# The fourth batch runs three steps behind the third in the second front block

## The chip, the cores and the metric

The kernel runs on one core of one Trainium2 chip. The metric is the device time of one execution in microseconds (us); lower is better. All data are float32, apart from a few small tables.

## What is computed

The reference is a stack of four layers over x (4 batches, 512 tokens, width 128), each with a gated cross-attention to a context of 32 tokens and a gated feed-forward part:

```python
x = x + tanh(g_xattn[0]) * L0_xattn(layernorm(x), ctx, ...)   # one head, 32 keys
x = x + tanh(g_ffn[0])   * L0_ffn(layernorm(x), ...)          # MXFP4 rounding, then one 128x128 product
x = x + tanh(g_xattn[1]) * L1_xattn(layernorm(x), ctx, ...)   # 16 heads, 32 keys
x = x + tanh(g_ffn[1])   * L1_ffn(layernorm(x), ...)          # router, top 2 of 8 experts
x = x + tanh(g_xattn[2]) * L2_xattn(...)                      # layers 2 and 3: the other 1,580 us
...
```

The change touches only the stage that computes the first three of these lines for the last two batches. The attention of layer 1 is the part that matters most below:

```python
scores = einsum('bqhd,bkhd->bhqk', q, k) / sqrt(8)            # 16 heads of 8
scores = where(mask == 0, -1e9, scores)
out = einsum('bhqk,bkhd->bqhd', softmax(scores), v)           # then @ Wo + bo
```

## The kernel before

The program is a sequence of blocks; all engines meet at the end of each. The first block computes the "front" (the three lines above) of batches 0 and 1 beside the setup. The **second front block**, `fronts_beside_route` (L3102 to L3123), computes the front of batch 2 (the third) and batch 3 (the fourth), and beside them the router of the first two batches, `route_1` with g = 0, whose last act is 16 indirect DMAs that scatter token rows to the experts' pages. The third block, `moe_1_pages`, works on those pages.

The order of every engine's queue is fixed by `interleave` (L749). Each part of the work is written, for each engine, as a generator that yields step numbers. The first part is the main one (here the third batch), the others are sides. Before the main part's code of a step, all sides with a due step no later than it are advanced, the lowest due first, and at equal dues the side named first. What the sides have left after the main part follows at the end. So with equal step numbers the fourth batch goes just ahead of the third at every step on every engine. The router runs at two front steps for one of its own; its 16 scatters (L1240) are due on POOL from step 20 in half steps.

Engines are in order: an instruction that waits holds all behind it. One front (`front`, L794) has these steps, by name of the product in PSUM: `kv` (0, from the context), `xt0` and `q0` (2, 3), `sc0` (5, scores of layer 0), `vo`, `vo1` (6, 7), `pt0`, `y0` (8, 9, output of layer 0's attention), quantisation on DVE (12 to 15, L416 to L434), `xt1`, `y1` (17, 18), `xt2`, `q1` (21, 22), and then the layer-1 attention over four token tiles t:

- `sc1_t` (23+t): PE makes the scores (L890), DVE takes them out of PSUM with a minimum (L1041) and reduces the maximum (L1044);
- POOL subtracts it (L1093, from step 23), ACT takes the exponential (L951, from 24), DVE sums and inverts (L1049 and L1050, from 25), POOL multiplies (L1098, from 25);
- `pt1_t` (27, 28, 30, 31): PE transposes (L898), ACT copies (L955);
- `v1_0` (29) and `v1_1` (32): PE multiplies by the values (L904, 16 products), DVE adds bias and residual (L1055, L1058).

A front has one PSUM bank, so each product of a batch waits until the one before it has been taken out (`free_for`, on the semaphore `taken`). The two fronts have banks and buffers of their own. In the trace the third batch's tiles are called rows, turned, small_f and x; those of the fourth weights, ysb, region_a, work and pt. Layer norms take statistics on DVE (L664, L667), an inverse root on POOL (L674, L675, `norm_rstd`, steps 0, 10, 19) and the application on DVE (L685). POOL also widens keys and values to all heads (L1074, L1079).

`paced` (L3066) wraps a side so that every step it yields goes through a function; it exists and is used in a later block.

Of the kernel before, what the change touches and what calls it, by code (L numbers as in the profile page):

```python
# [63 lines left out]
def record(**fields):  # L64

    return namedtuple("Record", fields)(**fields)


def flamingo_kernel(nc, a, at, early_at, out):
    with ExitStack() as ctx:  # L70
# [4 lines left out]
        def sems(parity, names, behind=None):  # L75

            first = behind.end if behind else 0
            for n in range(len(sem_sets[parity]), first + len(names)):
                sem_sets[parity].append(ctx.enter_context(nc.semaphore(f"{'even' if parity == 0 else 'odd'}_{n}")))
            return record(end=first + len(names), **dict(zip(names, sem_sets[parity][first:])))  # L80
# [17 lines left out]
        def bank(i, n=1):  # L98
            return psum[:, 512 * i:512 * (i + n)]
# [12 lines left out]
        def part(region, offset, shape):  # L112

            n = int(np.prod(shape[1:]))
            v = region[0:shape[0], offset:offset + n]
            if len(shape) == 3:
                v = v.rearrange("p (a b) -> p a b", a=shape[1])
            if len(shape) == 4:
                v = v.rearrange("p (a b c) -> p a b c", a=shape[1], b=shape[2])
            return v  # L120
# [194 lines left out]
        def next_inputs(n):  # L315
            return dict(ctx_tok=lg[0:K, 2 * n:2 * n + 2, :].rearrange("p t e -> p (t e)"), ctx_t=lge[:, n, 0:K],
                        mask0=lge[:, n, K:2 * K].bitcast(I32),
                        mask1=comb[:, 2 * n:2 * n + 2, :].rearrange("p t (h k) -> p (t h) k", h=2).bitcast(I32))

        front_3, front_4 = dict(front_1, **next_inputs(0)), dict(front_2, **next_inputs(1))  # L320
        w_at = front_tail + FRONT_SMALL
        front_w2 = record(stats=part(region_a, w_at, [P, T, 6]), mv=part(region_a, w_at + 24, [P, T, 2]),
                          rstd=part(region_a, w_at + 32, [P, T]), rtmp=part(region_a, w_at + 36, [P, T]),
                          rstd2=part(region_a, w_at + 40, [P, T]), xn=part(work, 0, [P, T, D]), xnt=part(wide_2, 3584, [P, S]))
# [87 lines left out]
        def over(ap, axis, shape):  # L412
            return ap.unsqueeze(axis).broadcast_to(shape)
# [349 lines left out]
        def block_of(k, sync, main, sides, first_loads=None):  # L763

            with nc.Block() as block:  # L765
                @block.sync
                def _(sp):
                    if first_loads:
                        first_loads(sp)
                    clear_set(sp, 1 - k % 2)  # L770
                    sync(sp)

                @block.tensor
                def _(pe):
                    interleave(main.tensor(pe), [side.tensor(pe) for side in sides])

                @block.scalar
                def _(act):
                    interleave(main.scalar(act), [side.scalar(act) for side in sides])

                @block.vector
                def _(dve):
                    interleave(main.vector(dve), [side.vector(dve) for side in sides])

                @block.gpsimd
                def _(pool):
                    interleave(main.gpsimd(pool), [side.gpsimd(pool) for side in sides])
# [461 lines left out]
        def load_pages(sp, s, q):  # L1249
            lo = 4 * P * (q % QUADS)  # L1250
            sp.dma_start(page_rows[:, q % 3, :, :],
                         sorted_1[q // QUADS][lo:lo + 4 * P, :].rearrange("(j p) d -> p j d", p=P)).then_inc((s.in_0, s.in_1, s.in_2)[q % 3], 16)
# [1813 lines left out]
        def paced(side, at_step):  # L3066

            def slowed(program):
                def of_engine(eng):
                    for n in program(eng):  # L3070
                        yield at_step(n)
                return of_engine
            return record(tensor=slowed(side.tensor), vector=slowed(side.vector), scalar=slowed(side.scalar),
                          gpsimd=slowed(side.gpsimd))
# [3 lines left out]
        def next_block():  # L3078
            block_at[0] += 1
            return block_at[0]  # L3080
# [21 lines left out]
        def fronts_beside_route():  # L3102
            k = next_block()
            sf = sems(k % 2, FRONT)
            sg = sems(k % 2, FRONT, sf)
            sr = sems(k % 2, ROUTE_1, sg)
            sw = sems(k % 2, ("table_in",), sr)
            s_pages = sems(1 - k % 2, PAGES_1)

            def sync(sp):  # L3110
                sp.wait_ge(sf.inputs, 5 * 16)
                sp.wait_ge(sg.inputs, 5 * 16)
                lo = early_at["b1"][0]
                sp.dma_start(w1[D - 1:D, :, 0:F1],
                             a["early"][0:E8, lo:lo + F1].rearrange("(o e) f -> o e f", o=1)).then_inc(sw.table_in, 16)
                lo = at["be2"][0]
                sp.dma_start(be2_rows[:, :, :], over(a["weights"][0:E8, lo:lo + D], 0, [P, E8, D])).then_inc(sw.table_in, 16)
                sp.wait_ge(sw.table_in, 32)
                sp.wait_ge(scattered_1[0], 16 * K1 * GT)
                for q in range(3):  # L3120
                    load_pages(sp, s_pages, q)
            block_of(k, sync, front(sf, 2, bank(0), front_3, set_f),
                     [front(sg, 3, bank(1), front_4, front_w2), route_1(sr, 0, bank(2), lambda n: 2 * n, 4)])  # L3123

        def moe_1_pages():
            k = next_block()
# [99 lines left out]

        fronts_beside_setup()
        fronts_beside_route()
        moe_1_pages()
        for b in range(B):  # L3230
# [122 lines left out]
```

## Time and profile before

| | us |
|---|---|
| median of 3 runs | 1809.48 |
| lowest, highest | 1801.71, 1815.31 |
| time of the profiled execution | 1816.59 |
| its span | 1814.8 |
| second front block in it | 115.7 to 230.1 |

The profiled execution was 7.1 us above the median of the runs. All stretches are in us from the start of its span. The engines are PE (matmul), PEld (its weight load), DVE (vector), ACT (scalar), POOL (GpSimd) and SP (which issues plain DMAs). The busy shares of the whole span say little here, since most of it lies in later blocks; what the change touches is one stretch of 114.4 us, and it has to be read by itself.

### The profile page before, as it was taken

How to read it: one execution, taken by the hardware profiler on the slowest of the kernel's cores; microseconds unless marked ns; L12 is line 12 of the kernel's file. 1: busy time of each engine (PE TensorE's matmuls, PEld its weight loads, DVE VectorE, ACT ScalarE, POOL GpSimd, SP SyncE). 2: the span in 40 equal slices, each digit the busy share in tenths (PEclk: the TensorE clock that was granted, in tenths of full speed). 3: DMA queues.
4: the chain of work that ended last, by engine and by line, in shares of the span. 5: the costliest groups of instructions: out<-in, count | busy, mean ns of one | idle time of the engine just before them, and what ended most of it. 6: DMA issues, size and time to landing. Idle time of an engine off the chain costs nothing. (4 is left out here: it accounts for less than half of the span.)

```text
span 1814.8 us, 30972 instructions
## 1 busy us (share of the span) xinstructions
PE 1594.1 (88%) x10175; PEld 1088.8 (60%) x10175; DVE 1175.5 (65%) x3120; ACT 772.7 (43%) x1974; POOL 850.9 (47%) x1075
## 2 busy tenths in 40 slices
PE   5655599899999999999999997968999999788799
PEld 4545376657756567655577564545656765567655
DVE  6867577857747467575577564476847757445557
ACT  2321244446627466355465273122226626533421
POOL 2551734538647277474486562011727647400072
PEclk7875799999999999999999997879999999899899
DMA  8200122100000400000000001014410000434363
GB/s 300 79 13 1 41 83 77 42 10 10 1 1 2 162 13 4 1 1 1 5 9 1 1 2 47 1 46 135 144 33 2 1 18 1 148 91 117 94 161 115
DMA packets 79564, 91.34 MB, mean 50 GB/s; under 512 B 10872, under 2 KB 57592, under 8 KB 78480
## 3 DMA queue, kind: packets, MB, share of 16 engines
q1 hardware_dynamic: 74288, 78.86, 13.9%
q0 software_dynamic: 5120, 10.50, 2.0%
q8 instruction: 86, 1.41, 0.3%
q14 instruction: 70, 0.57, 0.1%
HBM read 69.14 MB, written 27.66 MB: 53 GB/s over the span
## 5 line engine op out<-in xcount | busy, mean ns | idle before, releaser
L1677 POOL TENSOR_TENSOR rows<-rows,rinv 128x512 f32<-128x512 f32 x192 | 198.7, 1063 | 117.2 <-DVE rinv L1917 117.2
L1841 ACT ACTIVATE rows<-psum,nmax 128x512 f32<-128x512 f32 x192 | 130.0, 683 | 122.1 <-DVE nmax L1910 122.0
L2026 POOL TENSOR_TENSOR rows<-rows,rinv 128x128 f32<-128x128 f32 (+2 forms) x192 | 127.4, 685 | 76.5 <-DVE rinv L2195 76.5
L1909 DVE TENSOR_REDUCE lg<-psum 128x2 f32<-128x1024 f32 x128 | 155.7, 1217 | 3.2
L2190 DVE TENSOR_REDUCE nmax<-psum 128x1 f32<-128x128 f32 (+3 forms) x256 | 113.6, 486 | 41.7 <-PE psum L2072 40.7
L1921 DVE COPY turned<-psum 128x512 f32<-128x512 f32 x128 | 88.2, 689 | 80.3 <-PE psum L1737 79.3
L1725 PE MATMUL psum<-region_a,region_b 64*128 64x256 f32 x1024 | 130.6, 391 | 6.0 <-ACT rows L1841 2.9
L1758 PE MATMUL psum<-turned,region_a 128*64 128x256 f32 x1024 | 124.6, 385 | 0.4
L2069 PE MATMUL psum<-region_a,region_b 64*128 64x128 f32 (+2 forms) x896 | 105.9, 349 | 10.5 <-ACT rows L2142 4.6
L1725 PEld LDWEIGHTS psum<-region_a,region_b 64*128 64x128 f32 x1024 | 92.8, 186 | 28.9 <-ACT rows L1841 7.7
L1737 PEld LDWEIGHTS psum<-weights,rows 128*128 128x128 f32 x768 | 82.0, 140 | 44.9 <-issue 20.7
L1737 PE MATMUL psum<-weights,rows 128*128 128x128 f32 x768 | 103.3, 279 | 3.9 <-ACT turned L1850 2.4
L2142 ACT ACTIVATE rows<-psum,nmax 128x128 f32<-128x128 f32 (+2 forms) x192 | 96.1, 509 | 11.2 <-DVE nmax L2190 11.2
L2584 ACT ACTIVATE region_b<-psum 128x512 f32<-128x512 f32 x66 | 39.4, 598 | 139.7 <-PE psum L2546 139.7
L1758 PEld LDWEIGHTS psum<-turned,region_a 128*64 128x64 f32 x1024 | 68.6, 136 | 47.1 <-issue 19.6
L1850 ACT ACTIVATE turned<-psum 128x512 f32<-128x512 f32 x128 | 76.7, 599 | 46.0 <-PE psum L1737 46.0
L2069 PEld LDWEIGHTS psum<-region_a,region_b 64*128 64x128 f32 x896 | 69.4, 188 | 34.6 <-ACT rows L2142 11.9
L2558 PEld LDWEIGHTS psum<-region_c,region_b 128*128 128x128 f32 x512 | 66.0, 192 | 28.0 <-issue 22.7
L2084 PE MATMUL psum<-weights,rows 128*128 128x128 f32 x448 | 76.3, 280 | 6.6 <-DVE region_a L2201 1.4
L1703 PE MATMUL psum<-kvt,weights 128*128 128x512 f32 x128 | 66.1, 646 | 11.2 <-PEq L765 7.6
L2850 POOL DMA_INDIRECT sorted<-turned,small_f x48 | 49.2, 1024 | 49.6 <-DVE small_f L2784 35.2
L1689 POOL TENSOR_TENSOR ysb<-ysb,nmax 128x128 f32<-128x128 f32 x64 | 25.9, 405 | 94.8 <-DVE nmax L1910 93.9
(866 smaller groups left out, 3962.0 us busy)
## 6 DMA issues: line engine op xcount, KB each, us to landing
pt<-gates SPq DMA_DIRECT2D x64, 128.0 KB, 3.1
ysb<-gates SPq DMA_DIRECT2D x64, 128.0 KB, 3.1
weights<-sorted SPq DMA_DIRECT2D x28, 256.0 KB, 3.0
made<-weights SPq DMA_DIRECT2D x28, 256.0 KB, 2.3
sorted<-sorted SPq DMA_DIRECT2D x4, 1536.0 KB, 13.7
region_a<-in_eg SPq DMA_DIRECT2D x16, 256.0 KB, 4.4
region_a<-in_eu SPq DMA_DIRECT2D x16, 256.0 KB, 3.9
region_c<-in_weights SPq DMA_DIRECT2D x16, 256.0 KB, 5.7
```

The lines of the kernel that those rows point to most:

```text
L1677: nc.gpsimd.tensor_tensor(row(u, j), row(u, j), rinv[:, 2 * u + j:2 * u + j + 1].broadcast_to([P, S]), ALU.mult).then_inc(s.pn, 1)
L1725: mm = nc.tensor.matmul(s_bank(u, j)[:, 256 * half:256 * (half + 1)], qtt[lo:lo + 64, p, P * t:P * (t + 1)], ktt[lo:lo + 64, p, 256 * half ...
L1737: mm = nc.tensor.transpose(turn_bank(place(n, i))[:, P * k:P * (k + 1)], row(u, j)[:, P * k:P * (k + 1)], ident[:, :])
L1758: nc.tensor.matmul(bank(7)[lo:lo + HD2, 256 * half:256 * (half + 1)], vtok[:, k, P * p + lo:P * p + lo + HD2], turned2[:, 2 * half + j, k, :],
L1841: nc.scalar.activation(row(u, j), s_bank(u, j), ACT.Exp, bias=nmax[:, 2 * u + j:2 * u + j + 1], accum_out=sum_column(u // T, u % T, j)).th ...
L1850: nc.scalar.activation(turned_to(n, i), turn_bank(place(n, i)).rearrange("p (k q) -> p k q", q=P), ACT.Copy).then_inc(s.ca, 1)
L1909: link(nc.vector.tensor_reduce(maxima(u // T)[:, both(u), 0], both_scores(u), AX.X, ALU.max, negate=True))
L1921: nc.vector.tensor_copy(turned_to(n, i), turn_bank(place(n, i)).rearrange("p (k q) -> p k q", q=P)).then_inc(s.cb, 1)
L2026: nc.gpsimd.tensor_tensor(head, head, rinv[:, 2 * u + j:2 * u + j + 1].broadcast_to([P, keys(u)]), ALU.mult).then_inc(s.pn, 1)
L2069: nc.tensor.matmul(s_bank(u, j)[:, cols], qtt[lo:lo + 64, p, P * t:P * (t + 1)], krot[lo:lo + 64, cols], start=(h == 0), stop=True, skip_g ...
L2142: nc.scalar.activation(rows_of(u)[:, j, 0:keys(u)], s_bank(u, j)[:, 0:keys(u)], ACT.Exp, bias=nmax[:, 2 * u + j:2 * u + j + 1], accum_out= ...
L2190: nc.vector.tensor_reduce(nmax[:, 2 * u + j:2 * u + j + 1], s_bank(u, j)[:, 0:keys(u)], AX.X, ALU.max, negate=True).then_inc(s.mx, 1)
```

## The change

The fourth batch's front is wrapped in `paced` with `lambda n: n + 3`: on every engine but SP, its step n is due where the third batch's step n + 3 was. No instruction is added, removed or altered; only the order within the queues of PE, ACT, DVE and POOL is another.

```diff
@@ -3120,7 +3120,7 @@
                 for q in range(3):
                     load_pages(sp, s_pages, q)
             block_of(k, sync, front(sf, 2, bank(0), front_3, set_f),
-                     [front(sg, 3, bank(1), front_4, front_w2), route_1(sr, 0, bank(2), lambda n: 2 * n, 4)])
+                     [paced(front(sg, 3, bank(1), front_4, front_w2), lambda n: n + 3), route_1(sr, 0, bank(2), lambda n: 2 * n, 4)])
```

The POOL queue at the end of the block, by this rule (3 and 4 are the batches, D the scatters, sub L1093, mul L1098):

```
before: 4:rstd 3:rstd D0-D5 4:sub0 D6 3:sub0 D7 4:sub1 D8 3:sub1 D9 4:sub2 4:mul0 D10 3:sub2 3:mul0 D11
        4:sub3 4:mul1 D12 3:sub3 3:mul1 D13 4:mul2 D14 3:mul2 D15 4:mul3 3:mul3
after:  3:rstd D0-D3 4:rstd D4-D6 3:sub0 D7 D8 3:sub1 D9 D10 3:sub2 3:mul0 D11 4:sub0 D12 3:sub3 3:mul1
        D13 4:sub1 D14 3:mul2 D15 4:sub2 4:mul0 3:mul3 4:sub3 4:mul1 4:mul2 4:mul3
```

The ends of the other queues after the change:

```
PE:  3:pt1_0 4:sc1_2 3:pt1_1 4:sc1_3 3:v1_0 4:pt1_0 3:pt1_2 4:pt1_1 3:pt1_3 4:v1_0 3:v1_1 4:pt1_2 4:pt1_3 4:v1_1
ACT: 3:copy0 4:exp1 3:copy1 4:exp2 4:exp3 4:copy0 3:copy2 4:copy1 3:copy3 4:copy2 4:copy3
DVE: 3:sum2 4:max2 4:sum0 3:sum3 4:max3 4:sum1 3:v1_0 4:sum2 4:sum3 4:v1_0 3:v1_1 4:v1_1
```

## Rows read from the trace of the kernel before

**Rows 1.** The page, part 1: busy time, share and instructions of each engine.

```profile
PE 1594.1 (88%) x10175; PEld 1088.8 (60%) x10175; DVE 1175.5 (65%) x3120; ACT 772.7 (43%) x1974; POOL 850.9 (47%) x1075
```

**Rows 2.** Windows: stretch, length, busy time and count by engine, granted clock, DMA share.

```profile
115.70:230.10 114.40, 64.79 (x298) 48.37 (x298) 77.43 (x272) 23.02 (x49) 51.31 (x70) 0.67 0.07 21
...
115.70:158.60 42.90, 26.17 (x132) 20.87 (x132) 29.01 (x130) 9.67 (x26) 16.17 (x34) 0.63 0.05 13
158.60:182.00 23.40, 9.39 (x42) 8.93 (x42) 20.46 (x86) 1.40 (x3) 1.27 (x2) 0.57 0.00 0
186.20:222.80 36.60, 23.36 (x79) 13.16 (x78) 21.43 (x38) 10.26 (x17) 32.60 (x32) 0.74 0.09 29
```

**Rows 3.** Waits of DVE in the block: total us, times, longest.

```profile
DVE weights L1006 <- PE psum L858: 4.6, 1, 4.6
DVE kvt L1153 <- POOL kvt L1227: 3.7, 1, 3.7
...
DVE small_f L993 <- PE psum L839: 2.1, 1, 2.1
```

**Rows 4.** Timeline of POOL: start, duration, instruction; first scatter, last multiplication.

```profile
184.69 0.23 POOL L674 TENSOR_SCALAR rtmp_f<-mv_f 128x4 f32<-128x4 f32 x1 [3.68 <-DVE mv_f L667]
185.00 1.03 POOL L675 TENSOR_TENSOR rstd_f<-rtmp_f,neg_half 128x4 f32<-128x4 f32 x1
186.24 1.29 POOL L1240 DMA_INDIRECT sorted<-region_c,slots  x1 [0.20 <-issue]
...
221.69 1.05 POOL L1098 TENSOR_TENSOR rows<-rows,small_f 128x512 f32<-128x512 f32 x1
```

**Rows 5.** POOL's instructions by line, 182 to 223.5: busy us, mean ns, idle before.

```profile
L1240 POOL DMA_INDIRECT sorted<-region_c,slots x16 | 16.0, 1002 | 3.4 <-issue 3.4
L1093 POOL TENSOR_TENSOR rows<-rows,small_f 128x512 f32<-128x512 f32 x4 | 4.2, 1057 | 0.1
```

**Rows 6.** Timeline of DVE: quantisation's start, the third batch's step 18, the end.

```profile
158.51 0.68 DVE L420 TENSOR_REDUCE region_a<-y 128x16 f32<-128x512 f32 x1
...
181.94 0.69 DVE L1025 TENSOR_TENSOR turned<-psum,weights 128x512 f32<-128x512 f32 x1
...
184.52 1.08 DVE L685 TENSOR_SCALAR work<-weights,region_a 128x128 f32<-128x128 f32 x4
...
229.59 0.48 DVE L1058 SCALAR_TENSOR_TENSOR x<-turned,gate,x 128x256 f32<-128x256 f32 x1
```

**Rows 7.** Timeline of PE: transposes and value products at either clock.

```profile
215.19 1.12 PE L898 MATMUL psum<-weights,rows 128*128 128x128 f32 x4 [2.12 <-ACT turned L955]
216.10 3.39 PE L904 MATMUL psum<-weights,ysb 128*128 128x128 f32 x16
219.33 1.95 PE L904 MATMUL psum<-rows,turned 128*128 128x128 f32 x16
...
224.77 0.66 PE L898 MATMUL psum<-weights,rows 128*128 128x128 f32 x4 [0.25 <-ACT turned L955]
```

**Rows 8.** Timeline of ACT: an exponential and a copy.

```profile
214.02 0.63 ACT L951 ACTIVATE rows<-rows 128x512 f32<-128x512 f32 x1 [2.12 <-POOL rows L1093]
...
225.46 0.60 ACT L955 ACTIVATE turned<-psum 128x512 f32<-128x512 f32 x1 [0.26 <-PE psum L898]
```

**Rows 9.** Timeline of DVE: two operations, each once short and once long.

```profile
130.16 0.18 DVE L974 TENSOR_SCALAR pt<-region_a 128x32 f32<-128x32 f32 x1
...
131.57 0.97 DVE L974 TENSOR_SCALAR pt<-cap3s 128x32 f32<-128x32 f32 x1
...
219.99 3.04 DVE L1058 SCALAR_TENSOR_TENSOR weights<-pt,gate,weights 128x256 f32<-128x256 f32 x1
...
227.80 0.49 DVE L1058 SCALAR_TENSOR_TENSOR weights<-pt,gate,weights 128x256 f32<-128x256 f32 x1
```

**Rows 10.** Windows, columns as in rows 2: the granted clock late in the block.

```profile
206.00:210.00 4.00, 1.54 (x7) 0.76 (x5) 2.48 (x6) 0.63 (x1) 3.77 (x5) 0.50 0.05 16
...
222.00:226.00 4.00, 2.33 (x18) 2.03 (x19) 1.85 (x3) 1.97 (x4) 0.74 (x1) 1.00 0.65 191
```

## The prediction

> **What bounds the kernel now.** I began with the page. Its busy line [rows 1] shows PE busy for 88% of the span, but that is a mean over stages; the changed block is 114.4 us of 1814.8, so I cut it out with the windows view and left the rest. In the block [rows 2] no engine is full: PE 64.8 us, DVE 77.4, POOL 51.3, ACT 23.0. The later lines of that group cut it into three stages.
>
> - 115.7 to 158.6: DVE works 29.0 of 42.9 us. The 13.9 us in which it rests are chains through other engines: 3.7 us for POOL's iota at the start, 2.1 and 4.6 us for PE products [rows 3].
> - 158.6 to 182: DVE works 20.5 of 23.4 us. Quantisation of both batches and the router stand one behind the other; DVE is the bound.
> - 186.2 to 222.8: POOL shows 32.6 us of work in 36.6, and the rest is issue gaps between scatters (16.0 us of work and 3.4 of gaps for 16 of them [rows 5]). POOL is the bound. Its first scatter starts at 186.24 only because both inverse roots, the third batch's at 185.00, stand in front of it; its last multiplication starts at 221.69 [rows 4]. After that 7.3 us of transposes, copies and value products follow, up to 230.07 on DVE [rows 6].
>
> So the block's end is: DVE's work up to the layer norm of layer 1, then POOL's queue, then a tail.
>
> **The change, part by part.** Nothing is added, so all terms are changes of waits. I walk the four new queues with the durations of the rows.
>
> *First stage.* The router's iota now comes first on POOL, and DVE's 3.7 us wait for it shrinks to 0.7: 3.0 gained. The third batch's chain then runs without the fourth's to fill its waits: an inverse root costs 0.31 + 1.03 = 1.35 us from statistics to application [rows 4], now exposed twice (2.8 us with hand-overs), and some 0.8 us for the context's chain. Later the fourth's `sc0`, `vo` and `y0` each stand in PE's queue behind two to four products of the third and the router; I get DVE waits of 2.0, 3.1 and 3.0 us where the waits of before were 2.1, 0.7 and 4.6 [rows 3]. In all 13.9 us of waits (0.7, 2.8, 0.8, 8.1, and 1.5 of small ones) against 12.4 that I count by the same standard: with hand-overs about +1.7 us. This is the term I trust least. I bound it below by -3.7 (the whole wait for the iota falls away and nothing comes for it) and above by +4.6 (one more product wait as long as the longest).
>
> *Second stage.* DVE is full, so order costs nothing here. Before, DVE started quantising at 158.51 and reached the third batch's step 18 at 181.94 [rows 6], 23.4 us later, with the fourth's step 18 of 2.6 us and a wait of 1.3 us ahead of it. Afterwards the fourth's step 18 comes behind the third's and the wait is gone, so the third's step 18 starts at 158.5 + 1.7 + 23.4 - 2.6 - 1.3 = 179.7. Its 2.6 us (181.94 to 184.52) and the inverse root of 1.35 end at 183.7. POOL's first scatter starts there, at 183.9 with the hand-over: 2.3 us earlier than 186.24.
>
> *POOL's queue.* A scatter costs (16.0 + 3.4) / 16 = 1.21 us, a subtraction or multiplication 1.05 [rows 5]. From 183.9: four scatters (4.8), the fourth batch's inverse root (1.35), now inside this run, then twelve scatters (14.5) and thirteen tensor operations (13.7) up to the fourth's last subtraction: 218.3. I checked that inputs are there. The tightest is the fourth's last maximum: PE makes its `sc1_3` only behind the third's `pt1_1`, which needs mul1 of the third at about 208.8, so the maximum is ready near 212.5 and POOL asks for it at 217.2. 4.7 us of cover hide that link; if they are gone, each us goes to the end. Three multiplications remain, to 221.4, against 222.7 before: POOL is done 1.3 us earlier.
>
> *The tail.* Here the lag is paid. ACT's queue holds the fourth's exp3 in front of its copy0 and of the third's copy2, so no `pt1` after the first of the fourth leaves PSUM before 218.3 + 0.63 (exp) + 0.60 (copy0) = 219.6 [rows 8]. Then in PE's order: the fourth's pt1_1 (1.1 at the low clock), the third's pt1_3 (1.1), the fourth's v1_0 (3.4 low), the third's v1_1 (1.95 high) [rows 7], which ends near 227.3. Then alone, with nothing beside them: pt1_2 0.66, copy 0.60, pt1_3 0.66, copy 0.60, v1_1 1.95, DVE's two operations 0.95, and five hand-overs of about 0.1. Sum 227.3 + 5.4 + 0.3 = 233.0, against 230.1. The tail behind POOL's last operation grows from 7.3 to 11.6 us.
>
> SP's page loads of the next block wait for the last scatter, which comes about 6 us earlier. That is worth nothing, since PE starts the next block at the meeting of the engines.
>
> **Sum.** POOL's start: +1.7 (first stage) -2.6 -1.3 (the fourth's step 18 and the wait, no longer ahead) = -2.2, with hand-overs -2.3. The inverse root inside the run: +1.35. The 0.4 us that POOL waited before its first subtraction: -0.4. So POOL's end: -1.3. The tail: 11.6 - 7.3 = +4.3. Together +3.0, and 233.0 against 230.07 is +2.9; I take +2.9. Against the profiled execution, 1816.59 + 2.9 = 1819.5; against the median of the runs, which lay 7.1 us lower, 1809.5 + 2.9 = **1812.4 us**.
>
> **Clock.** The granted clock was 0.50 (1.2 GHz) from 206 to 210, where PE worked 1.5 of 4 us, and 1.00 (2.4 GHz) from 222 to 226 [rows 10]; the first 16 value products took 3.39 us, the next 1.95 [rows 7]. I let the first `v1` of the closing run be slow and the rest fast, as there. With all of the tail fast the end is 2.4 us earlier (+0.5 instead of +2.9), with all of it slow 3.8 later (+6.7). The Trainium skill (TensorE: Matmul & The Clock Gate, Part 1) says that a gate halves the array's clock depending on how busy PE has been; by that rule the thinner PE work of a lagged tail speaks for the slow side, and the trace agrees (0.50 in the thin stretch).
>
> **Rivals.**
>
> *The lag pays (faster by a few us).* POOL is the bound of the last stage and starts 2.3 us earlier; if the tail overlaps well, only the fourth's pt1_3, copy, v1_1 and DVE's part follow its last multiplication (0.66 + 0.60 + 1.95 + 0.95 + hand-overs = 4.6): 221.8 + 4.6 = 226.4, so -3.7, 1805.8 us. For it: POOL at 32.6 of 36.6 us [rows 2]. Against it: ACT's order, exp3 ahead of copy0. A second mechanism speaks against it: DVE operations on SBUF alone were stretched while POOL ran tensor operations, 0.18 to 0.97 us and 0.49 to 3.04 us [rows 9]. The third's `v1_0` addition (L1058) would now fall into POOL's densest run with the fourth's sum2 and sum3 behind it; a stretch of 3 us brings POOL's end to about 224.8 and this rival to -0.7 us. In my own sum it is hidden, since PE asks for the fourth's mul3 only near 228.6. The Trainium skill (GPSIMD Engine Reference, Key points) says that GpSimd shares its SBUF interfaces with VectorE and contends with VectorE instructions that have two SBUF inputs or a 2-port mode; the trace agrees with both long rows.
>
> *The queues lock each other (clearly slower).* The place is PE's queue at the third's pt1_1 and the fourth's sc1_3, with DVE's `v1_0` ahead of sum2. It decides once the fourth's last maximum is later than 217.2, that is once more than 4.7 us are lost: then POOL stands idle. The price is what is over that, plus the slow tail (3.8): +6 to +10 us, 1815.5 to 1819.5. A cap for it: if the lag were pure addition, three steps of 33 in 114.4 us are 10.4 us.
>
> *No lag in time.* The order changes, but where every queue waits for the same chains both batches finish as before: within 1 us, 1809.5. For it: 77.4 us of DVE work in 114.4 is the same work; against it: the change in POOL's and ACT's order is real.
>
> **How the numbers follow.** Chances: my sum (+1 to +6) 0.50; the lag pays 0.20; lock 0.17; no shift 0.13. With the first stage at -3.7 instead of +1.7 and a fast tail my sum is 2.9 - 5.4 - 2.4 = -4.9; with +4.6 and a slow tail it is 2.9 + 2.9 + 3.8 = +9.6. And the three runs lay 7.8 us below to 5.8 above their median, so a median can be off by some 4 either way. From 1809.5 - 4.9 - 4 = 1800.6 to 1809.5 + 9.6 + 2 = 1821: I take 1801 to 1821. One per cent, about what a measurement can tell from no change, is 18.1 us; no case reaches it, with 10.4 the largest. So within 1% has 0.93; 0.03 faster and 0.04 slower are left for effects in later blocks that I do not see.
>
> **What would show it.** Right: the first scatter near 184, POOL's last multiplication between 221 and 223, the block's end near 233, a tail of 10 us or more after POOL, and ACT's copy of the fourth's first transposes directly behind its exp3. A first scatter later than 186.2 would put the first-stage term wrong; gaps over 1 us in POOL's run would show the lock; an end before 229 would show that the lag pays. The whole is wrong if blocks after 233 change by more than the shift itself.

## The result, and the profile after

The changed kernel took 1819.15 us (median of 13 runs, 1814.03 to 1822.42); the kernel before, now with 13 runs on the same chip, 1800.85 us (1798.39 to 1815.31). The ratio, over which the interval is given, is 1.0072 (95%: 1.0047 to 1.0098): 13 us slower, 8.5 to 17.6. The two medians themselves lie 18.3 us apart, so the size on this chip is not well known. On another chip a second comparison gave 1.0045 (1.0017 to 1.0073), or 8.6 us of 1912.7. The time lies in the forecast range and within 1%, but the forecast shift was 2.9 us and the measured one is three times that on the later chip and more than four times on the first.

The windows view of the changed kernel, first the block, then the stretches that answer to those of [rows 2] (columns: stretch, length, busy us and count of PE, PEld, DVE, ACT, POOL, granted clock, DMA share, GB/s). The block runs from the last DVE operation of the first block, 114.13, to PE's first product of the next at 232.54.

```profile
114.10:232.50 118.40, 74.61 (x298) 54.20 (x298) 80.02 (x272) 22.87 (x49) 51.53 (x70) 0.61 0.07 21
114.10:157.00 42.90, 30.78 (x127) 25.18 (x128) 26.46 (x116) 9.37 (x25) 15.13 (x32) 0.54 0.05 13
157.00:180.30 23.30, 10.44 (x43) 8.74 (x42) 20.79 (x89) 1.57 (x4) 1.26 (x2) 0.50 0.00 0
184.50:223.50 39.00, 25.46 (x74) 13.31 (x75) 27.39 (x52) 10.74 (x18) 33.86 (x34) 0.68 0.15 48
```

By the same marks the block took 230.38 - 115.70 = 114.7 us before and 232.54 - 114.13 = 118.4 after: +3.7. The mean granted clock fell from 0.67 to 0.61; in the second stage it was 0.50 throughout. PE's busy time rose by 10 us for the same products. The timeline of POOL in the changed kernel shows the earliest scatter and the end of its queue:

```profile
184.56 1.29 POOL L1240 DMA_INDIRECT sorted<-region_c,slots  x1 [0.20 <-issue]
...
219.15 1.03 POOL L1098 TENSOR_TENSOR weights<-weights,region_a 128x512 f32<-128x512 f32 x1
221.43 2.05 POOL L1098 TENSOR_TENSOR weights<-weights,region_a 128x512 f32<-128x512 f32 x2 [1.25 <-DVE region_a L1050]
```

The first scatter stands 70.4 us into the block; in [rows 4] it was 70.5. POOL ends at 109.4 instead of 107.0, and it waited 1.25 us for DVE ahead of its last two multiplications. The timeline of DVE shows why:

```profile
215.24 0.42 DVE L1055 TENSOR_TENSOR turned<-psum,weights 128x256 f32<-128x256 f32 x1 [0.42 <-PE psum L904]
215.70 4.77 DVE L1058 SCALAR_TENSOR_TENSOR x<-turned,gate,x 128x256 f32<-128x256 f32 x1
220.39 0.67 DVE L1049 TENSOR_REDUCE region_a<-weights 128x16 f32<-128x512 f32 x1
```

The addition of the third batch's `v1_0` took 4.77 us while POOL ran tensor operations (such an addition took 0.49 us in [rows 9] when POOL was done), and the fourth's sum2 stood behind it.

### The profile page after: what moved, and what is told of

Same layout as the page of the kernel before. It is cut to its first block and busy times, and to the rows that moved or that the text cites. A ratio compares the mean times of both kernels' runs of the same rounds, so it can differ in the third digit from the quotient of the medians.

```text
span 1813.0 us, 30977 instructions
## 1 busy us (share of the span) xinstructions
PE 1598.5 (88%) x10175; PEld 1090.4 (60%) x10175; DVE 1177.9 (65%) x3120; ACT 771.6 (43%) x1974; POOL 847.1 (47%) x1075
## 5 line engine op out<-in xcount | busy, mean ns | idle before, releaser
L2142 ACT ACTIVATE rows<-psum,nmax 128x128 f32<-128x128 f32 (+2 forms) x192 | 96.0, 509 | 11.6 <-DVE nmax L2190 11.6
L2850 POOL DMA_INDIRECT sorted<-turned,small_f x48 | 49.1, 1023 | 50.8 <-DVE small_f L2784 36.5
L2545 PE MATMUL psum<-xnt,region_a 128*128 128x512 f32 x128 | 68.0, 613 | 2.9 <-DVE region_b L2622 2.9
```

What stands on the lines that cost most here:

```text
L2142: nc.scalar.activation(rows_of(u)[:, j, 0:keys(u)], s_bank(u, j)[:, 0:keys(u)], ACT.Exp, bias=nmax[:, 2 * u + j:2 * u + j + 1], accum_out= ...
```

## Experiments

All figures of a block are counted from the last DVE operation of the first block to PE's first product of the next one. The kernels below ran on three other chips than the first comparison; there every kernel, the one before included, is about 100 us longer (last section), so only ratios and blocks are compared. A block is read from one profiled execution. The intervals of all kernels with three steps of lag overlap, so the ratios do not rank them.

| kernel | block us | ratio to before | 95% interval |
|---|---|---|---|
| before, three profiles | 114.7, 110.7, 110.7 | | |
| lag 3, three profiles | 118.4, 118.9, 118.8 | 1.0045 | 1.0017 to 1.0073 |
| lag 1, two profiles | 110.1, 110.0 | 0.9985, 0.9970 | 0.9962 to 1.0007, 0.9951 to 0.9989 |
| lag 3 early only | 121.1 | 1.0047 | 1.0024 to 1.0071 |
| lag 3 late only | 114.3 | 1.0014 | 0.9989 to 1.0038 |
| lag 3, PE filled from 158 us | 118.5 | 1.0039 | 1.0012 to 1.0065 |
| lag 3, PE filled at the start | 118.0 | 1.0032 | 1.0017 to 1.0046 |
| lag 3, addition from PSUM | 118.3 | 1.0027 | 1.0009 to 1.0044 |
| before, end delayed | 117.7 | 1.0026 | 1.0011 to 1.0040 |

### Is the profile of before typical, and does a later block pay?

The block had become 3.7 us longer between the two profiles at hand, the kernel 13 us by the runs. Two theories: later blocks answer to the shift through TensorE's clock, which changes often in them (A), or the front blocks themselves vary and the profile of before was an unlucky sample (B). Both kernels were profiled again, unchanged.

> The kernel before, unchanged, for one more profile of it. Its 13 runs fall into two groups, 9 of 1798.4 to 1801.7 us and 4 of 1807.9 to 1815.3, and the profile at hand is of the second. Theory A (the block costs 4 us and later blocks answer to the shift through TensorE's clock): a profile of the 1800 group has the second front block as long as before, 114 us within 1, and is shorter somewhere between 1100 and 1240 us, where the granted clock changes often. Theory B (the front blocks themselves vary): the difference lies before 240 us.

> The changed kernel once more, for a profile of its commoner group (9 of 13 runs at 1818.8 to 1822.4; the profile at hand is of 1814.8). Theory A: the second front block stays at 118 us within 1, and the extra 4 to 6 us lie behind 1000 us. Theory B: they lie before 240 us.

Measured: before took 110.7 us for the block, after 118.9. Theory A's expectation of "114 us within 1" for before failed: the block itself varies by 4 us in the kernel before. The length of 114.7 us is called the long form below, that of 110.7 the short form. In three profiles of the changed kernel it doesn't vary (118.4 to 118.9). The windows of 146 to 158 us and of the whole block in this second profile of before:

```profile
116.00:226.70 110.70, 60.34 (x298) 44.59 (x298) 76.47 (x272) 22.73 (x49) 51.45 (x70) 0.69 0.07 22
146.00:158.00 12.00, 8.27 (x63) 7.62 (x61) 8.28 (x36) 3.12 (x7) 3.28 (x6) 0.78 0.00 1
```

The same stretch in the first profile of before:

```profile
146.00:158.00 12.00, 10.56 (x61) 9.43 (x60) 6.76 (x31) 3.52 (x7) 3.28 (x6) 0.64 0.00 0
```

And in the changed kernel, in its third profile:

```profile
115.90:234.80 118.90, 75.28 (x299) 55.78 (x300) 78.64 (x274) 22.82 (x49) 51.62 (x70) 0.61 0.07 20
146.00:158.00 12.00, 11.75 (x53) 10.10 (x51) 4.54 (x22) 2.73 (x6) 2.02 (x4) 0.50 0.00 0
```

Between 146 and 158 us the clock was 0.78 in the short form of before, 0.64 in the long form, 0.50 with the lag. A third profile asked which form comes again:

> The kernel before once more, for a third profile of it. From the end of the first block, its second front block took 114.4 us in one profile and 110.4 in the other; the first 114 us of the delayed kernel, which has the same order, are a third sample with the long form. Expected: one of the two forms again, 110 to 115 us, and which one goes with how long PE was granted the full clock around 148 to 155 us (3.4 us of it in the long form, about 7 in the short one).

It was the short form, 110.7 us, with 0.78 in that stretch:

```profile
116.20:227.00 110.80, 61.36 (x299) 45.58 (x300) 76.48 (x274) 22.72 (x49) 51.38 (x70) 0.68 0.07 22
146.00:158.00 12.00, 8.49 (x64) 7.84 (x62) 8.28 (x37) 3.12 (x7) 3.27 (x6) 0.78 0.01 1
```

Against the short form the lag costs 8.1 us within the block, not 3.7. Which form is the commoner isn't shown. Both short profiles are of executions near the lower end of their kernel's runs (1904.1 us with a median of 1911.3, and 1906.8 with 1912.6), and the run with the delay below, which has the same order, shows the long form on one of these chips too.

The two forms part in two places. The first scatter comes at 70.5 us of the block in the long form and at 68.8 in the short one: 1.7 us. The other 2 us lie in the tail (7.3 us against 5.3). There the fourth's first addition (L1058) took 3.04 us beside POOL's last scatter and multiplications in the long form [rows 9], and the third's next transposes waited for the DVE operation behind it. In the short form, 1.7 us earlier, the addition took 0.49 us and there was no such wait. Timelines of PE in the first profile of before, and of DVE in the second:

```profile
223.42 0.66 PE L898 MATMUL psum<-weights,rows 128*128 128x128 f32 x4 [1.71 <-DVE turned L1055]
```

```profile
217.66 0.49 DVE L1058 SCALAR_TENSOR_TENSOR weights<-pt,gate,weights 128x256 f32<-128x256 f32 x1
```

Theory A still held in part: a later block varies too. From one and the same DVE instruction to another (L2221 at 1099.1 us to L2419 at 1176.5 in the first profile of before), with the same work, windows of the first and the second profile of before, and of the second and third of the changed kernel:

```profile
1099.10:1176.50 77.40, 63.38 (x230) 36.31 (x231) 33.51 (x122) 20.43 (x32) 9.01 (x20) 0.78 0.08 27
```

```profile
1101.30:1170.70 69.40, 55.91 (x231) 32.54 (x231) 33.58 (x123) 20.42 (x32) 9.01 (x20) 0.85 0.10 31
```

```profile
1109.70:1185.50 75.80, 61.83 (x230) 35.60 (x231) 33.52 (x123) 20.42 (x32) 9.00 (x20) 0.80 0.09 28
```

```profile
1108.50:1177.80 69.30, 55.76 (x230) 32.33 (x231) 33.51 (x122) 20.45 (x32) 8.99 (x20) 0.85 0.09 31
```

So the first profiled execution, 16 us over the median of 13 runs, holds 8 us in this one later stretch, at a lower clock, that the second doesn't. And 6.5 us there account for the 6.3 us between two executions of the changed kernel (1925.4 and 1919.0), behind 1000 us as its expectation had it. On the later chips the stretch took 69.3 or 69.4 us in all five profiles with the old order or one step of lag, and 69.3 to 77.4 us in the seven with some lag of three; in the first chip's profiles it was 77.5 before and 71.0 after. That is too few to say whether the lag makes the long form likelier.

### The shift without the reordering

```diff
                     interleave(main.scalar(act), [side.scalar(act) for side in sides])
+                    link = chained(act, delayed)
+                    for _ in range(act_tail):          # 11 in the second front block
+                        link(nc.scalar.activation(work[:, :], cosq3[:, :], ACT.Copy))
```

> The order of before, with 11 copies on the idle end of ScalarE's queue in the second front block, one waiting for the other, so that the block ends about 3.7 us later (116 to 118.5 us instead of 114.4) with nothing reordered. Extra work: the copies, whose result nobody uses. Theory A (shift): the time rises by much more than the shift, +13 us and within 4 of the changed kernel (1815 to 1823). Theory B (order): it rises by the shift alone, to 1803 to 1806 us.

```profile
224.20 7.23 ACT L783 ACTIVATE work<-weights 128x512 f32<-128x512 f32 x11
```

The copies took 7.23 us, and the block ended at 117.7 where DVE's own work was done at 114.1. The kernel before has 0.3 us between the two, so the end is 3.3 us later for nothing but a delay. The ratio was 1.0026, +5.0 us (2.1 to 7.6): within the noise, a later end of this block costs what it is late, or up to some 4 us more. The stretch from 1099 us of above took 69.3 us here. The 13 us of the shift theory are outside the interval: that theory fell, on this chip.

### The lag in one half only

```diff
-  [front(sg, 3, bank(1), front_4, front_w2), ...
+  [paced(front(sg, 3, bank(1), front_4, front_w2), lambda n: n + 3 if n < 17 else n), ...   # lag_early
+  [paced(front(sg, 3, bank(1), front_4, front_w2), lambda n: n if n < 17 else n + 3), ...   # lag_late
```

> The changed kernel again, timed beside the kernel before on this chip. Expected from the 13 runs of either on record: ratio 1.005 to 1.010, +8 to +18 us. Theory A (clock and tail): the second front block takes 118 us in it, against 110 to 114 in profiles of before. Theory C (the cost lies behind the block): the block is 114 to 116.

> The fourth batch is three steps behind only up to the quantisation (steps under 17); from step 17 on the order is that of before. Theory A1 (the cost is in the first stage: PE is never granted the full clock between 118 and 196 us): the first scatter comes 70 us after the block's start, the block takes 112 to 114 us, the total is 2 to 5 us over before. Theory A2 (the cost is in the tail alone): the block takes 110 to 111 us and the total is within 2 us of before.

> The order of before up to the quantisation; from step 17 on (layer norm of layer 1, its attention) the fourth batch is three steps behind. Theory A1: the first stage is that of before, so the first scatter comes at 66 to 67 us of the block; with the long tail it takes 113 to 115 us, +3 to +5 us in all. Theory A2: nearly all of the loss is here, 116 to 118 us, +8 or more.

The repeated lag of 3 met its expectation only in part: the block was 118.8 us, the ratio 1.0045, a little under what had been named. The early half took 121.1 us, far over both theories. The late half took 114.3, within theory A1's 113 to 115, but with a first scatter at 64.9 where 66 to 67 had been named. Milestones, in us from the block's start:

| | third's y0 taken | fourth's y0 taken | first scatter | POOL ends | DVE ends |
|---|---|---|---|---|---|
| before, long form | 38.4 | 36.5 | 70.5 | 107.0 | 114.4 |
| before, short form | 36.8 | 35.0 | 68.8 | 105.1 | 110.4 |
| lag 3 | 35.0 | 43.8 | 70.4 | 109.4 | 118.1 |
| lag 3 early | 34.9 | 43.8 | 77.1 | 113.5 | 120.8 |
| lag 3 late | 36.7 | 34.9 | 64.9 | 103.9 | 114.0 |
| lag 1 | 33.7 | 35.5 | 66.3 | 102.4 | 109.7 |

The early lag makes the fourth's `y0` 7 to 9 us later, and with the old order behind it both inverse roots still stand ahead of the scatters, so the first scatter comes as late: 77.1, 8.3 us behind the short form. The late lag lets the third's root pass alone and wins 4 us there (64.9), and then gives them back: 39.0 us from first scatter to POOL's end against 36.3, and 10.1 us of tail against 5.3. The early half costs 10.4 us against the short form, the late half 3.6, both together 8.1: they don't add up, since the late half frees the first scatter of the fourth's late root (70.4 instead of 77.1). What stays of the early half is 5.5 us at the first scatter (70.4 instead of 64.9). Both halves cost, and that the first scatter of the full lag comes where the long form of before has it (70.5) is chance.

### Is it the clock or the order?

Products whose results nobody uses were put where PE waited.

```diff
+                for step, products in products_at:
+                    yield step
+                    for _ in range(products):
+                        nc.tensor.matmul(bank(4), ident[:, :], cosq3[:, :], start=True, stop=True)
+  # lag3_busy: [(0, 5), (12, 5), (15, 3), (16, 3), (20, 3), (23, 1), (25, 1), (26, 1)]
+  # lag3_warm: [(0.5, 7), (4.9, 2)]
```

> The changed kernel with 22 products of 128x512 whose results nobody uses, put into PE's queue where it waited (5 at the start, 11 before the fourth's xt1, 3 before xt2, 3 among the scores). Theory A1 (clock): PE is granted the full clock for most of 118 to 196 us, products there take half, and the block falls from 118 to 113 to 116 us although PE has more to do. Rival (the waits are set by order alone): the block stays at 118 or grows by some us with the extra products.

```profile
114.50:158.00 43.50, 35.71 (x140) 27.66 (x140) 26.43 (x115) 9.41 (x25) 15.16 (x32) 0.58 0.05 13
158.00:182.00 24.00, 19.77 (x65) 10.38 (x64) 22.09 (x90) 1.68 (x4) 1.26 (x2) 0.86 0.00 1
```

The clock rose from 0.50 to 0.86 between 158 and 182 us and the block stayed at 118.5: DVE is the bound there (22.1 of 24 us), and a faster PE is worth nothing. Up to 158 us the clock had hardly changed (0.58 against 0.54). So this run tells only of the second stage. The next put the filling ahead of the first.

> The changed kernel with 9 idle products of 128x512 in PE's queue, 7 ahead of the third's first transposes, where PE waited 7.6 us, and 2 ahead of the fourth's, where it waited 2.6. Their results are used by nobody. The earlier filling changed the clock only from 158 us on, where DVE is the bound, and won nothing. Clock theory: the full clock now comes before 150 us, the router's logits take 2 us instead of 3.4, the fourth's y0 comes at 41 us of the block instead of 43.8, the first scatter at 68 instead of 70.4, the block takes 115.5 to 117 us instead of 118.8. Order theory: y0 stays at 43 to 44.5 and the block at 118 to 119.5.

```profile
115.90:125.00 9.10, 7.28 (x24) 3.64 (x25) 6.33 (x36) 0.82 (x4) 2.76 (x13) 1.00 0.15 43
125.00:146.00 21.00, 15.78 (x73) 11.19 (x73) 15.67 (x58) 6.50 (x17) 10.38 (x16) 0.80 0.03 9
146.00:158.00 12.00, 11.75 (x52) 10.60 (x51) 4.45 (x21) 2.05 (x5) 2.02 (x4) 0.50 0.00 0
```

The clock was full at first, 0.80 up to 146 us where it had been 0.50, and back at 0.50 from there on, so the logits still took 3.42 us. The fourth's `y0` came at 42.9 instead of 43.8, the first scatter at 69.5, the block at 118.0: 0.8 to 0.9 us won, where the clock theory wanted 2 to 3. The rest of the first stage's loss is the order's, or the clock's between 146 and 158 us. What the fast clock between 146 and 158 us would give the lagged order wasn't reached, and its share stays open; an estimate from the durations of two products is 1.9 to 2.4 us (next section).

### DVE's long addition

This kernel leaves the output bias of layer 1's attention out of the result.

```diff
-  nc.vector.tensor_tensor(acc_f[:, rows, :], bk[...], over(bo1[:, :], 1, [P, 2, D]), ALU.add).then_inc(s.taken, 1)
-  dve.wait_ge(s.taken, made[f"v1_{half}"])
-  nc.vector.scalar_tensor_tensor(out=x[:, rows, :], in0=acc_f[:, rows, :], ...)
+  nc.vector.tensor_tensor(acc_f[:, rows, :], bk[...], over(bo1[:, :], 1, [P, 2, D]), ALU.add)
+  nc.vector.scalar_tensor_tensor(out=x[:, rows, :], in0=bk[...], ...).then_inc(s.taken, 1)
```

> The changed kernel in which DVE's last addition of layer 1's attention (L1058) takes the product from PSUM instead of the sum with the bias from SBUF. It leaves the output bias of that attention out of the result (all four batches); the number of instructions is the same. Port theory: the 4.8 us that this addition took while POOL ran tensor operations fall to 0.5, POOL's wait of 1.25 us ahead of its last two multiplications goes, POOL ends at 107.7 us of the block instead of 109.0, the block is 0 to 1.5 us shorter than 118.8, since the tail behind it is bound by PE and ACT. If the addition still takes over 2 us, something other than its second SBUF operand held it.

The timelines of DVE and of POOL in it:

```profile
216.17 0.48 DVE L1057 SCALAR_TENSOR_TENSOR x<-psum,gate,x 128x256 f32<-128x256 f32 x1
```

```profile
215.78 1.05 POOL L1093 TENSOR_TENSOR weights<-weights,region_a 128x512 f32<-128x512 f32 x1
216.78 1.04 POOL L1098 TENSOR_TENSOR weights<-weights,region_a 128x512 f32<-128x512 f32 x1
...
219.79 3.04 POOL L1098 TENSOR_TENSOR weights<-weights,region_a 128x512 f32<-128x512 f32 x3
```

With one of its two tensors in PSUM the addition took 0.48 us beside the same POOL operations. POOL's last three multiplications ran without a gap and ended at 108.1 us of the block instead of 109.4. The block took 118.3 us, at most 0.6 less than the three profiles with the lag (118.4 to 118.9): the tail is bound by PE and ACT, as expected. The same edit to the order of before, where the long addition did hold up PE in the long form, wasn't run.

### One step of lag

> The fourth batch one step behind the third instead of three. Theory A: the block is about 1 us longer or equal (114 to 116), and the total is wherever that shift puts it, 1800 to 1806 if small shifts do nothing. Theory B (each step of lag costs a third of 18 us): 1805 to 1808.

> One step of lag again, timed longer, since it is the only order tried whose block was shorter (110.1 us against 110.7 in the better profile of before) and whose ratio was below one (0.9985, interval 0.9962 to 1.0007). Expected: ratio 0.997 to 1.001. If one step is a real gain it is at most the 4 us between the two forms of before (0.998); if not, 1.000.

The block took 110.1 and 110.0 us, slightly shorter than even the short form of before. The ratios were 0.9985, which can't be told from one, and 0.9970 (0.9951 to 0.9989), 5.7 us faster. The first expectation (a block of 114 to 116 us, and a time from that of before to some 7 us over it) was on the wrong side; the second (0.997 to 1.001) held at its edge. The windows of the second profile:

```profile
115.40:225.40 110.00, 67.19 (x298) 50.40 (x298) 76.23 (x272) 23.01 (x49) 51.09 (x70) 0.66 0.07 22
144.00:156.00 12.00, 9.89 (x56) 8.93 (x55) 6.94 (x36) 3.41 (x7) 2.53 (x4) 0.64 0.00 1
```

The third goes just ahead instead of just behind, the router's iota no longer waits for the fourth's statistics, and the fourth's `y0` is at 35.5 us, not at 43.8. DVE waited 0.69 us for the iota instead of 3.72. POOL ends 2.7 us earlier than in the short form (102.4), and the tail gives 2 us of that back (7.3). Between 144 and 156 us the clock was 0.64 here, as in the long form, and the block was still the shortest: the clock there doesn't set the length alone. This is the best version found. It is clearly faster than three steps of lag; that it is faster than the kernel before rests on one of two timings.

## Why the prediction was right and where it failed

**The direction held, and most of the way; the block's end is in part luck.** The walk of the four queues put the block's end at 117.3 us from its start (233.0 - 115.7); the changed kernel's DVE ended at 118.1. But this small miss of 0.8 us is three larger ones that cancel: the first scatter 2.2 us later than forecast, POOL's queue 1.4 longer, the tail 2.8 shorter. The fourth's `sc0`, `vo` and `y0` brought DVE waits of 2.50, 2.81 and 4.31 us, forecast as 2.0, 3.1 and 3.0. ACT's copy0 stood directly behind exp3, as the tail's argument said. Timeline of ACT in the changed kernel:

```profile
219.22 0.63 ACT L951 ACTIVATE weights<-weights 128x512 f32<-128x512 f32 x1 [2.36 <-POOL weights L1093]
219.75 0.58 ACT L955 ACTIVATE ysb<-psum 128x512 f32<-128x512 f32 x1
220.23 0.59 ACT L955 ACTIVATE turned<-psum 128x512 f32<-128x512 f32 x1
```

**The step that failed is the base.** "Against the profiled execution, 1816.59 + 2.9 = 1819.5; against the median of the runs, which lay 7.1 us lower" took the block of the one profiled execution as the block of the kernel. It was the long form: 114.7 us where two other profiles have 110.7. The sum of waits was made against a sample whose clock was lower between 146 and 158 us (0.64, not 0.78) and whose tail held a long addition; the three profiles of the lagged order all have 0.50 there. 8.1 us is the lag's cost against the short form, 3.7 against the long one. The measured 8.6 us (3.3 to 14.0) on the later chip fits either. The 13 us (8.5 to 17.6) on the first chip are 5 us more than the block shows against the short form and 9 more than against the long one. The shift experiment, on another chip, speaks against the shift alone as their cause, and no profile of the short form exists from the first chip. The later stretch that takes 69 to 77 us by itself can add or hide as much. This rest stays open.

The median of three runs was a weak base as well. The prediction let a median be off by 4 us either way (and used only 2 of them above); with 13 runs it fell by 8.6, to 1800.85. That the time of 1819.15 lies only 7 us from the 1812.4 named is luck: the base was 8.6 us too high, and the shift 10 us too small by the ratio, 15 by the medians.

**First stage, forecast +1.7 us:** the first scatter was to come at 68.2 us of the block (183.9) and came at 70.4. Of DVE's waits, the three named ones came to 9.6 us instead of 8.1, and 0.7 more are in the others (DVE waited 1.21 for the third's own `y0`). The walk had used durations of before's own timeline, where the logits and the fourth's `y0` ran partly or wholly at the full clock. In the changed kernel they ran at the low one. Timeline of PE in the changed kernel:

```profile
150.85 3.42 PE L1127 MATMUL psum<-weights,region_c 128*128 128x8 f32 x16
...
155.82 2.07 PE L858 MATMUL psum<-region_a,ysb 32*128 32x128 f32 x8 [0.25 <-ACT ysb L934]
```

In the first profile of before the logits took 2.48 us, in the second 1.95; the fourth's `y0` 1.15. 0.94 and 0.92 us of these two groups of products, both ahead of the fourth's `y0` on DVE, are an estimate of the clock's part in the 2.2 that were missed; no run raised the clock there to test it. In the prediction's paragraph on the clock only the tail was given a low and a high price; the first stage needed it too.

**POOL's queue, forecast 37.5 us from the first scatter to the end:** it took 38.9. The inverse root inside it was priced right. The 1.25 us that it waited for DVE came through L1058, 4.77 us instead of 0.49. The mechanism stood in the prediction, as what takes the gain from a rival, with 3 us and the words "In my own sum it is hidden"; as far as the block's end goes that was right, since taking the long addition away moved it by 0.6 us at most. What the prediction missed is that such an addition, 3.04 us in its own rows, stood on the way to the end of the block it started from. The Trainium skill (GPSIMD Engine Reference, Key points) has GpSimd contend with VectorE instructions that have two SBUF inputs; the experiment agrees: 4.77 us with two of them, 0.48 with one.

**The tail, forecast 11.6 us:** it took 8.8. PE's chain of the fourth's pt1_1, the third's pt1_3 and the two value products took 6.3 us (220.39 to 226.73) instead of 7.7: the full clock came back within the fourth's `v1_0`, which took 2.76 us, not 3.4, and the two groups of transposes started 0.90 us apart, not 1.1. Another 1.3 us are no gain: POOL's last multiplications were late by that much and PE didn't need them yet, so less was left to count behind them. (The sum also names five hand-overs of 0.1 us and adds 0.3.) Against the long form that is +1.4, against the short form (5.3 us) +3.5.

**The rivals.** "The lag pays" saw that the tail has room and that POOL could start earlier; with the lag late only, POOL did start at 64.9, but the tail ate it. "The queues lock each other" names +6 to +10 us, where the 8.6 us of the later chip lie, but not for its reason: the fourth's last maximum was ready at 213.9 and used at 218.15, 4.2 us of cover where 4.7 had been forecast. The gap of over 1 us in POOL's run, named as its sign, did come (1.25 us), through DVE's long addition ahead of sum2 and not through PE's queue, and it didn't reach the block's end. "No lag in time" is refuted by the milestones. Of the other signs, the tail of 10 us or more didn't come in these profiles (8.8 to 9.2). And behind the block the two executions of the first chip differ by 3.9 us (1584.4 before, 1580.5 after), more than the block's own 3.7 and the other way; the stretch from 1099 us alone, 77.5 and 71.0, is more than that.

## What to carry to other kernels

A stretch of many short products whose clock changes can have more than one length with nothing altered, so a small change to it needs more than one profile of the kernel before. Compare the execution's own time with the median first, look for such stretches outside the change too, and price matmuls at both clock levels in every stage, not in the tail alone. One step of lag won or cost nothing here, three cost 4 to 8 us of the block: two chains that fill each other's waits can be moved too far apart. A lag shifts work from a shared middle to a lone end, and that end is to be counted in full.

## What the runs showed of the hardware

- A DVE addition with two SBUF tensors took 4.77 us, for 0.49 us of work, while POOL ran five tensor operations one behind the other, and ended 0.3 us after them; with one input in PSUM it took 0.48 us beside them. In the kernel before it took 3.04 or 0.49 us by where POOL's queue stood, in one and the same order.
- PE's work in one and the same order took 64.8 or 60.3 us in the block (PE busy, before, long and short form), and the block 114.7 or 110.7. The two differ in the stretches in which the full clock was granted and in the long addition; which of them starts the difference isn't shown. A later stretch of the same work took 77.4 us at a mean clock of 0.78 or 69.4 at 0.85.
- On the later chips each execution was about 100 us longer. The first and second profile of before stay within about 6 us of each other up to 1240 us; then long waits of DVE and ACT appear, of DVE for the DMAs that bring the gates of the experts (`pt` and `ysb`), between 1240 and 1345 us and again behind 1700. The waits of DVE from 1240 to 1345 us in the second profile, of which 31.7 us is a single one:

```profile
DVE region_b L2630 <- remote: 45.6, 4, 31.7
```

What held these transfers isn't shown. Waits of this kind (34.7 to 48.2 us for this line) stand in the profiles of all kernels on those chips and in neither of the first chip.
